# Six stages of a decoder kernel joined into three programs: mixer one beside the end of attention, mixer two beside the end of the state space

## The reference, cut to what matters

```python
x = _layernorm(x + attention(x))                              # stage 1: 16 heads of 16
x = _layernorm(x + mixer(ctx, ctx, x, ssm_kernel, D))         # stage 2: mixer one
x = _layernorm(x + ffn_ternary(x))                            # stage 3: FFN one, int8-like rounding, sign(W)
x = _layernorm(x + mamba2(x))                                 # stage 4: state space (SSD)
x = _layernorm(x + mixer(x, k, skip, ctx, ctx))               # stage 5: mixer two
x = _layernorm(x + ffn_hadamard(x))                           # stage 6: FFN two, w_gate, w_up, w_down ternary

# a mixer: 128 tokens = 16 heads h of 8, convolution (by fft) along the 256 features:
kv  = k[:, h, i, :] * v[:, h, j, :]           # all 8 x 8 pairs (i, j)
y   = causal_conv(kv, kernel) + skip * kv
out[j] = sum_i y[i, j] * q[i]
```

## Time and profile before

| | us |
|---|---|
| median of 3 runs | 851.48 (851.45 to 851.56) |
| the profiled execution | 852.26 |
| its span, first to last instruction | 850.4 |
| PE busy | 753.7 |
| DVE busy | 639.4 |
| POOL busy | 479.8 |
| ACT busy | 397.5 |

### The profile page before, as it was taken

One profiled execution on the slowest core, in us unless ns is written; L12 is line 12 of the kernel. 1 busy time (PEld: TensorE's weight loads), 2 busy tenths in 40 slices (PEclk: granted clock), 3 DMA queues, 4 the chain that ended last, 5 costly groups with the idle time before them and its releaser, 6 DMA issues. The chain is left out here.

```text
span 850.4 us, 13389 instructions
## 1 busy us (share of the span) xinstructions
PE 753.7 (89%) x4390; PEld 511.3 (60%) x4414; DVE 639.4 (75%) x1291; ACT 397.5 (47%) x640; POOL 479.8 (56%) x660
## 2 busy tenths in 40 slices
PE   6999999969999698899689999975999859999895
PEld 5777777734443375677367777763444326777674
DVE  4667777736999776574579999972799978988874
ACT  2555555652000245543287778851000025777785
POOL 1112333346774444341237777796677359899993
PEclk9999999989999799999699999987999969999998
DMA  7800000021000500000021221103000000000001
GB/s 262 350 2 2 1 2 2 2 77 72 1 0 0 189 2 1 1 1 2 3 99 54 71 76 51 50 1 109 6 0 0 1 2 1 1 14 20 13 20 38
DMA packets 12579, 33.96 MB, mean 40 GB/s; under 512 B 2656, under 2 KB 8032, under 8 KB 11232
## 3 DMA queue, kind: packets, MB, share of 16 engines
q1 hardware_dynamic: 12512, 33.11, 10.8%
HBM read 30.94 MB, written 2.16 MB: 39 GB/s over the span
## 5 line engine op out<-in xcount | busy, mean ns | idle before, releaser
L1058 PE MATMUL ss_b<-XT,win_late 128*128 128x256 f32 x320 | 88.8, 410 | 4.5 <-DVE ss_xc L1274 4.1
L466 POOL TENSOR_TENSOR at_kbd<-at_qk,at_hmask 128x512 f32<-128x512 f32 x16 | 16.7, 1041 | 111.6 <-DVE at_qk L393 111.6
L583 PE MATMUL m_y<-m_kv,toep 128*128 128x512 f32 x128 | 67.9, 612 | 10.6 <-POOL m_kv L572 10.6
L572 POOL TENSOR_TENSOR m_kv<-XT,CTXT 128x1024 f32<-128x1024 f32 x32 | 61.6, 1949 | 24.6 <-PE m_y L585 21.6
L603 DVE TENSOR_REDUCE MIX<-m_pr 128x128 f32<-128x1024 f32 x64 | 74.7, 1210 | 0.0
L572 POOL TENSOR_TENSOR m_kv<-CTXT 128x1024 f32<-128x1024 f32 x32 | 59.8, 1893 | 24.4 <-PE m_y L585 22.1
L1058 PEld LDWEIGHTS ss_b<-XT,win_late 128*128 128x128 f32 x320 | 59.0, 200 | 19.1 <-DVE ss_xc L1274 11.4
L1274 DVE SCALAR_TENSOR_TENSOR ss_xc<-ss_b,cw_late,ss_xc 128x254 f32<-128x254 f32 x144 | 66.6, 477 | 4.7 <-ACT ss_xc L1164 1.2
L584 PE MATMUL m_y<-m_kv,toep 128*128 128x512 f32 x128 | 67.1, 607 | 0.0
L585 PE MATMUL m_y<-m_kv,toep 128*128 128x512 f32 x128 | 66.4, 601 | 0.0
L1552 PE MATMUL f_b<-had_last,f_ht 128*128 128x256 f32 x256 | 61.8, 385 | 0.0
(11 more groups left out here) (233 smaller groups left out, 1934.2 us busy)
## 6 DMA issues: line engine op xcount, KB each, us to landing
MIX<-cum_rows SPq DMA_DIRECT2D x16, 512.0 KB, 3.7
toep<-toep_dram SPq DMA_DIRECT2D x2, 2048.0 KB, 12.7
X<-x_dram SPq DMA_DIRECT2D x1, 2048.0 KB, 12.7
MIX<-wgu_dram SPq DMA_DIRECT2D x1, 2048.0 KB, 7.9
CTXT<-ctxT_dram SPq DMA_DIRECT2D x1, 2048.0 KB, 18.3
ctx_last<-ctx_dram SPq DMA_DIRECT2D x1, 2048.0 KB, 8.8
out_dram<-f_o SPq DMA_DIRECT2D x16, 128.0 KB, 1.7
XT<-xT_dram SPq DMA_DIRECT2D x1, 1280.0 KB, 8.4
```

Source lines behind the costliest of these rows:

```text
L466: nc.gpsimd.tensor_tensor(KBD[n % 2][:, :, :, :], QK[n % 3][:, 2:4, :].unsqueeze(2).broadcast_to([P, 2, 2, S]), hmask[:, :].unsqueeze(1).u ...
L572: m = nc.gpsimd.tensor_tensor(KV[k][:, c, :, :].rearrange("p (b j) i -> p b j i", b=B), ki, vj, ALU.mult)
L583: nc.tensor.matmul(bY[k][0][h][:, :], toep[:, a, 0:P], kv[0], start=True, stop=True)
L1058: m = nc.tensor.matmul(bX[(NU * g + n) % 3][:, 0:GS_], win[:, h, off:off + P], XT[:, h, bass.ts(g, GS_)], start=(h == 0), stop=(h == C - 1))
```

## The change

Each stage no longer makes its own block: it returns functions that emit one step of each engine's list. Three programs are built from them. The first holds attention and mixer one, the second FFN one, the state space and mixer two, the third FFN two. `interleave` puts the steps of a later stage between the last steps of an earlier one:

```diff
+def interleave(first, n_first, second, n_second, start, each=1):
+    done = 0
+    for i in range(max(n_first, start + n_second)):
+        if i < n_first:
+            first(i)
+        if i >= start:
+            for k in range(done, min(done + each, n_second)):
+                second(k)
+            done = min(done + each, n_second)
...
+            start, na = B + 2, B + 8
...
+                    interleave(at.tensor(pe), na, m0.tensor(pe), NI, start, 2)
+                    step = at.scalar(act)
+                    for i in range(na):
+                        step(i)
+                    m0.scalar(act)
+                    interleave(at.vector(dve), na, m0.vector(dve), NI, start, 2)
+                    interleave(at.gpsimd(pool), na, m0.gpsimd(pool), NI, start, 2)
...
+                nf, n_head, n_space, heads_at, mix_at = B + 9, NU, NG + 5, B + 3, NG
...
+                        step, head = st.tensor(pe)
+                        interleave(f0.tensor(pe), nf, head, n_head, heads_at)
+                        interleave(step_from(step, 1), n_space - 1, m1.tensor(pe), NI, mix_at - 1, 2)
...
+                        step, head = st.scalar(act)
+                        interleave(f0.scalar(act), nf, head, n_head, heads_at)
+                        for i in range(1, n_space):
+                            step(i)
+                        m1.scalar(act)
...
+                        step, head = st.vector(dve)
+                        interleave(f0.vector(dve), nf, head, n_head, heads_at)
+                        interleave(step_from(step, 1), n_space - 1, m1.vector(dve), NI, mix_at - 1, 2)
...
+                        for i in range(nf):
+                            f0_step(i)
+                        interleave(st.gpsimd(pool), n_space, m1.gpsimd(pool), NI, mix_at - 1, 2)
```

A mixer now has 32 items: half the sequences of one head each (16 heads for the first eight sequences, then 16 for the others). An item has two POOL instructions of 512 elements, three matmuls into two banks of one of three sets, two DVE products and one reduction over both halves of the features, which is put one item behind:

```diff
+        def step(n):                                   # gpsimd
+            h, a = divmod(n, HM)
...
+            if not skip and a == 0:
+                pool.wait_ge(before["x_kept"], HB * (h + 1))
+            upto(pool, s["conved"], n - 2)
...
+        def step(n):                                   # tensor
+            a = n % HM
+            if skip and n == 0:
+                pe.wait_ge(before["shifted"], 4 * B)
+            if skip and n == 2:
+                pe.wait_ge(before["back_kept"], B)
+                pe.wait_ge(before["ct_kept"], B)
+            if not skip and n == 0:
+                pe.wait_ge(before["tapped"], CC * NG)
+                pe.wait_ge(before["sz_made"], 4 * NG)
+            if not skip and n == 1:
+                pe.wait_ge(before["xs_kept"], B)
+            if not skip and n == 2:
+                pe.wait_ge(before["cbm_made"], B)
+                pe.wait_ge(before["y1_made"], B)
+            pe.wait_ge(s["kv_made"], n + 1)
+            upto(pe, s["multed"], 2 * n - 4)
...
+            if skip and n == 24:
...
+                nc.tensor.matmul(banks[0][:, 0:3], T["ones"][:, :], T["wpart"][:, :], start=True, stop=True).then_inc(s["totalled"], 1)
...
+        def step(n):                                   # vector
+            times_q(n)
+            if n:
+                add_up(n - 1)
+            if skip and n == 25:
...
+                nc.vector.reciprocal(T["inv_w"][:, :], T["wscale"][:, :]).then_inc(s["scales"], 1)
+            if n == NI - 1:
+                add_up(n)
```

The rounding of FFN two's weights leaves FFN one. It is done by ACT at the end of mixer one's list, and the clip on POOL and the subtraction are replaced by one Sign pass:

```diff
+        for k in range(3):
+            nc.scalar.activation(staged[k], staged[k], ACT.Identity, scale=T["inv_w"][:, k:k + 1], bias=T["rnd"][:, :]).then_inc(s["rounded"], 1)
...
+            nc.scalar.activation(dst, T[("wg1", "wu1", "wd1_raw")[k]][:, :, :], ACT.Sign, bias=T["unrnd"][:, :])
```

In the state space, group 0's ten units are the "head", of which one follows each step of FFN one from i = 19 on. Step 0 is left out, and `dt` and what hangs on it go to step 1, behind all ten units of the head:

```diff
+        def step(i):                                   # tensor
+            if i == 1:
+                front()                                # the dt products and transposes
             unit(i, 0)
             scan(GB * (i - 2) + 1)
+            if i > 1:
+                c_times_b(GB * (i - 1))
...
+            if i == 1:
                 pe.wait_ge(s["ones_set"], 1)
                 pe.wait_ge(math, 15)
...
+                c_times_b(0)
...
+        def head(k):
+            unit(0, k)
...
+            if i == 1:                                 # scalar, behind tap3(i, 5)
+                floor(0)
+                decay(0)
+                floor(1)
...
+            if i == 1:                                 # vector
+                front()
             taps(i, 0)
```

More of the change, by code:

```diff
@@ L44, in held, with run, step_from @@
     eng.sem_inc(passed, 1)
[L47 to L55, removed]
+Stage = namedtuple("Stage", "sync tensor scalar vector gpsimd")
+def interleave(first, n_first, second, n_second, start, each=1):
[7 more added lines that the diff above has]
+            done = min(done + each, n_second)
+def run(step, n):
+    for i in range(n):
+        step(i)
+def step_from(step, first):
+    return lambda i: step(first + i)
 class Chip:
@@ L1150, in _, with unit @@
-        @block.scalar
-        def _(act):
+        def unit(g, n):
+            if not 0 <= g < NG:
+                return
+            kind, r = UNITS[n]
+            if n == 0:
+                pe.wait_ge(before["x_kept"], GB * (g + 1))
+            if g == 0 and n == 0:
+                pe.wait_ge(before["later_in"], 160)
+            if g == 0 and n < 3:
+                pe.wait_ge(before[("silu1_made", "p1_made", "p0_made")[n]], B)
+            back = NU * g + n - len(bX)
+            if back >= 0:
+                if UNITS[back % NU][0] == "x":
+                    pe.wait_ge(s["tapped"], CC * (back // NU) + back % NU + 1)
+                else:
+                    pe.wait_ge(s["sz_made"], 4 * (back // NU) + back % NU - CC + 1)
+            off = DI + P * r if kind == "x" else P * r
+            for h in range(C):
+                m = nc.tensor.matmul(bX[(NU * g + n) % 3][:, 0:GS_], win[:, h, off:off + P], XT[:, h, bass.ts(g, GS_)], start=(h == 0), stop=(h == C - 1))
+            m.then_inc(s["unit_made"], 1)
@@ L1152, in _, with scalar, front @@
+        def head(k):
+            unit(0, k)
+        return step, head
+    def scalar(act):
+        def front():
             nc.scalar.activation(ea[:, :], T["a_log"][:, :], ACT.Exp)
@@ L1238, in _, with head, vector, front @@
+        def head(k):
+            if k == 0:
+                act.wait_ge(before["later_in"], 160)
+            if k < CC:
+                tap3(0, k)
+            else:
+                gate(0, k - CC)
+                if k == CC + 1:
+                    silu(0)
+        return step, head
+    def vector(dve):
+        def front():
             dve.wait_ge(dt_made, 1)
```

2875 lines of the change are left out of this document (1456 added, 1419 removed).

## The result

The changed kernel takes 848.75 us (median of 20 runs, 845.21 to 852.98) against 852.25 for the kernel before on the same chip: ratio 0.9964, interval 0.9952 to 0.9975. By the ratio it is about 3.1 us faster, where 9.3 were forecast. The profiled execution has a span of 847.2 against 850.4.

A forecast was written before the change was run, and what follows sets the result against it. PE bounds a mixer's middle; the change's worth was read at stage ends and drains. 8.7 + 10.6 - 7 - 3 = 9.3 us gain took the median from 851.48 to 842 us; eight-in-ten range 826 to 849.

The forecast's parts named there:

- Part D: Mixer two beside the state space's drain: three PE pauses cancel what the barrier saves; loss of 3 us taken.
- part B: Rounding out of FFN one: ACT passes and POOL clips go, with the excess between Silus; gain 10.6 us.
- A: Mixer one beside attention's drain: PE starts its items earlier and stays the bound; gain 8.7 us.
- C: State space's head in FFN one's drain: dt products behind all ten units delay the chain; loss of 7 us taken.
- FFN two: Last stage, after mixer two: its list is the same, so it was forecast unchanged.
- PE's pause of 1.4 us: Attention's drain: PE stands about 1.4 us because DVE does items 0 and 1 before what context_turn(15) needs.
- the excess of the twelve intervals: FFN one's first Silus: 88.97 us instead of 78.6; the 10.3 us difference taken whole as the rounding's cost.
- the six ACT passes: Rounding in FFN one: passes of about 2.1 us each, going to mixer one, where ACT is idle.
- The ring: State-space head in FFN one's drain: units, turns, copies and taps wait on each other in a circle, 3.8 us per turn.
- Pauses of 4, 2.5 and 4.7 us: Mixer two's start in the state space's drain: PE idles three times between its first six items, waiting for POOL's products.
- the rivals: Whole kernel: overlap works as drawn, 823 (0.2); joins cost more than rounding gives, 856 (0.07); only rounding's removal counts, 841 (0.13).

The follow-up runs named there:

- a_serial: Changed kernel with mixer one's items moved behind attention's last step on all engines, same program; 852.84 us, ratio 1.0000 to the kernel before.
- b_twice: Changed kernel with six extra ACT passes over 2048 elements in FFN one where the rounding stood, no POOL clips; 849.72 us, ratio 0.9979.
- b_clips: Changed kernel with six extra ACT passes in FFN one and a POOL clip between each two; 858.77 us, ratio 1.0070.
- c_old: Changed kernel with the state space's head in the old order behind FFN one's last step, without a barrier; 843.55 us, ratio 0.9896.
- c_late: Changed kernel with the whole state-space head behind FFN one's last step, dt products still last; 845.90 us, ratio 0.9918.
- d_warm: Changed kernel with ten extra unread matmuls on PE in the three pauses before mixer two's items 0, 2 and 4; 845.33 us, ratio 0.9905.
- d_serial: Changed kernel with mixer two's items behind the state space's last step on every engine, same program; 834.26 us, ratio 0.9784.
- c_split: Changed kernel with head units 0 to 2 beside FFN one's drain, then the dt products, then the other seven units; 845.53 us, ratio 0.9921.
- both: Changed kernel with the state-space head in the old order and mixer two's items behind the state space's last step; 826.67 us, ratio 0.9697.

## Why the prediction went wrong

The gain came out 6.2 us smaller than forecast. Part D is 5.8 us worse than its term in the sum and part B 1.2 worse; A is 0.5 better, C and FFN two 0.2 each.

**A, right.** Forecast 8.7, measured 9.2. PE's pause of 1.4 us was 1.99, and FFN one starts at 270.7 where 271 was named. `a_serial` shows that I had the sum right and its make-up only partly: 3.1 to 4.4 us are the overlap, the rest comes with the join and the smaller items.

**B, right in sum, 1.2 us over.** I measured the excess of the twelve intervals against 6.55 us; without rounding six of them take 6.78, so 1.3 us of the 10.3 never belonged to it. The working also set the six ACT passes first. By `b_twice` and `b_clips` they are the small part, and the clips with POOL's waits for ACT the large one.

**C, right in sum, partly by luck.** The `dt` products came 31.5 us after the last first Silu (forecast 29), `scan(1)` 60.3 (forecast 60). The ring shows as drawn, but with three waits for taps of about 2.5 us (the third at 401.02) and two turns of 4.28 and 4.98 us instead of 3.8, at a granted clock of 0.50 to 0.56 from 392 to 404. The working had set 3 us for that and taken 0.8; the products came 2.5 late. From them to `scan(1)` it was 28.8 us instead of the 30.6 worked out, and that hid the first error: 1.7 of the 1.8 is that the `dt` products now ran at full clock, 1.92 us instead of 3.64. `c_old` confirms the loss, `c_late` that it has two halves of about 4 us.

**D, the step that failed.** The order of events and the pauses were right nearly to the tenth. On `scan(1)`'s shift of -11.77, items 0 and 1 were forecast at 575.6 and started at 563.90 + 11.77 = 575.7. Pauses of 4, 2.5 and 4.7 us were forecast; they are 4.04, 2.58 and 4.60. What failed is the step "After such pauses its clock may be the lower one ... each time that costs 2.2 ... I take a loss of 3". Three times 2.2 is 6.6, and the trace has it whole. Items 0 and 1 took 572.24 - 563.90 = 8.34 us instead of 5.14, item 2 took 4.30 and item 4 4.23 instead of 2.57: 3.2 + 1.7 + 1.7 = 6.6. `d_warm` gives 5.0 of it back. I had the price from mixer one's start, and a row in which PE was busy 3.56 of 4 us and still at a clock of 0.50, and took less than half as a hedge. Nor is the price one number: read in the same way, mixer two's start in the kernel before was 598.85 - 590.41 = 8.4 us, 3.3 over 5.15, as items 0 and 1 then cost. The other 2.2 of 8.8 are in the traces too. The two pairs of `x_turn`s behind items 5 and 7 take 605.48 - 604.35 = 1.13 us each, with a wait of 0.51 in the middle, where 0.4 a pair was worked out: 1.5 us. The barrier before FFN two took 1.3 us instead of 0.7 (678.61 - 677.31, 681.56 - 680.84): 0.6. That leaves 0.2 us at most, although two norms beside POOL's products took 1.07 and 1.15 us instead of 0.38.

**What the forecast did not ask.** Part D was weighed as overlap against the old serial order with a barrier. The third order, one program and no overlap, was not among the rivals. It was 15.3 us better than the order chosen, and its terms stood in the profile before: POOL done before PE in the drain, 5.7 us between `x_turn` and the first product. A rival of that form would also have told that half of A's gain or more comes without overlap.

## What to carry to other kernels

When two stages are fused, price the join (no barrier, the next stage's first producer started by its own semaphore) apart from the overlap, and take the order that does the join alone as a candidate: work laid into a drain whose chain runs through all engines delays that chain on each engine's list. Count a lower-clock start in full for every pause of TensorE that the forecast itself names. An instruction that waits for another engine's late work, put into the list of an engine that otherwise does tiny links of a chain, can cost its wait as well as its length (here a clip of 1.89 us among roots: 0.4 us behind a wait of 3.12, 2.7 to 4.4 behind one of 5.19), while passes of the same length on an engine with slack cost little.

## What the runs showed of the hardware

TensorE's clock fell behind pauses of 2.58 us, and behind pauses of 1.99 us in some executions only. It also fell without any such pause: in `d_serial` PE was busy 0.82 us of 573 to 575 and 0.85 of 575 to 577, with no wait over 0.60 us, and the granted clock of the next 2 us was 0.50. The profiles of eleven kernels have the same pause of 1.99 or 2.00 us in attention's drain. In five of them mixer one takes 94.0 us from its first pass to FFN one's first product, in six it takes 95.7. PE's timeline of `c_split`, one of the six, behind that pause, where the changed kernel has 1.02 for the same passes:

```profile
185.10 0.44 PE L266 MATMUL bank<-ident,at_cn 128*128 128x128 f32 x2 [1.99 <-DVE at_cn L416]
185.37 1.02 PE L618 MATMUL bank<-m_kv,toep 128*128 128x512 f32 x2
186.24 1.86 PE L619 MATMUL bank<-m_kv,toep 128*128 128x512 f32 x2
```

The granted clock from 186 to 188 us was 0.57 in `c_split` and 1.00 in the changed kernel. These 1.7 us can be a part of the changed kernel's spread of 845 to 853 us; `both` has the pause too and spread by 0.4 us in four runs, so it is not shown to be all of it.

A DVE norm with one tensor input from SBUF takes 1.07 to 1.15 us beside POOL products of 1.04 and 0.38 alone, as in the earlier trace rows. The Trainium skill, "GPSIMD Engine Reference", section 1, names DVE instructions in a two-port mode or with two SBUF inputs as those that contend; no run here shows which mode the norm was in. `gated`, which has two SBUF inputs, took 1.67 us at 447.73 beside a POOL instruction of 1.90 in the kernel before, and 0.69 at 577.90 in the changed kernel with none beside it: that agrees.
